# Three components of an edge vector, read as 96 rows of their own in the message stage of a four-layer graph network

## The reference

```python
sender, receiver = edge_index
s, v = node_feats[:, :32] @ W_up_s, einsum('nui,uw->nwi', node_feats[:, 32:].reshape(n, 32, 3), W_up_v)
tpw = silu(silu(edge_feats @ A1 + b1) @ A2 + b2) @ A3        # four weights of 32 for each edge
w0, w1, w2, w3 = split(tpw, 4)
ss, vs = s[sender], v[sender]
y_s, y_v = edge_attrs[:, :1], edge_attrs[:, 1:4]             # a scalar and three vector components
out_s0 = ss * y_s * w0
out_s3 = einsum('eui,ei->eu', vs, y_v) / sqrt(3) * w3
out_v1 = ss[:, :, None] * y_v[:, None, :] * w1[:, :, None]   # the three components, each times 32 channels
out_v2 = vs * y_s[:, :, None] * w2[:, :, None]
message = segment_sum(concat(out_s0, out_s3, out_v1, out_v2), receiver) / 10
out = message @ W_out                                        # scalar and vector parts with their own weights
```

## Time and profile before

| what | value |
|---|---|
| time before, median of 3 runs | 3766.24 us (3753.16 to 3766.95) |
| span of the profiled execution, the only time that it has | 4163.4 us |
| PE busy | 2637.4 us, 63% |
| PE weight loads | 1689.0 us, 41% |
| DVE busy | 1800.3 us, 43% |
| ACT busy | 1103.2 us, 26% |
| POOL busy | 2178.9 us, 52% |
| moved by DMA | 872.83 MB, mean 210 GB/s |
| message stage | about 2,990 to 3,690 us of the span |

### The profile page before, as it was taken

How to read it: one execution, slowest core, us unless ns; L and a number is a source line. 1 busy time by engine, 2 the same in 40 slices (tenths; PEclk the granted TensorE clock), 3 DMA queues, 4 the chain that set the end, 5 groups by cost and what they waited for, 6 DMA issues and landing times. The chain is left out here.

```text
span 4163.4 us, 41911 instructions
## 1 busy us (share of the span) xinstructions
PE 2637.4 (63%) x11696; PEld 1689.0 (41%) x11696; DVE 1800.3 (43%) x4207; ACT 1103.2 (26%) x2880; POOL 2178.9 (52%) x1937
## 2 busy tenths in 40 slices
PE   1547973665563648964555564359667786759696
PEld 1324653454452335643444442234323343334343
DVE  6433433554453544434444453320246685650203
ACT  0113430222232614421222233410224453430001
POOL 4357556666675757566666675620156577520000
PEclk9965555777776865556766777679778897869797
DMA  9997996777774549996777773537245564527372
GB/s 314 364 291 279 395 338 183 234 227 232 218 206 118 95 148 332 394 311 180 219 232 220 222 185 89 152 98 282 92 125 147 141 180 136 140 73 292 114 288 100
DMA packets 672304, 872.83 MB, mean 210 GB/s; under 512 B 136977, under 2 KB 557144, under 8 KB 631524
## 3 DMA queue, kind: packets, MB, share of 16 engines
q1 hardware_dynamic: 314324, 581.00, 39.8%
q0 software_dynamic: 118784, 157.05, 16.1%
q10 hardware_dynamic: 239008, 132.59, 10.8%
HBM read 441.21 MB, written 429.28 MB: 209 GB/s over the span
## 5 line engine op out<-in xcount | busy, mean ns | idle before, releaser
L1716 POOL DMA_INDIRECT att_rows<-table,kvrow x784 | 796.0, 1015 | 400.9 <-issue 230.3
L1484 POOL DMA_INDIRECT matrix<-count,place x392 | 621.5, 1585 | 279.2 <-DMA matrix<-count,place 196.9
L2119 POOL DMA_INDIRECT msg_rows<-rows,msg_src x392 | 411.4, 1050 | 448.6 <-DMA msg_src<-in_src_pt 218.1
L1774 PE MATMUL att_po<-att_message,att_mate 128*128 128x264 f32 (+1 forms) x1568 | 438.3, 419 | 300.0 <-issue 199.4
L1774 PEld LDWEIGHTS att_po<-att_message,att_mate 128*128 128x128 f32 x1568 | 296.1, 232 | 400.6 <-issue 324.9
L1607 PE MATMUL tab_bank<-wk,tab_kv 32*128 32x256 f32 x1600 | 378.6, 686 | 74.3 <-DVE tab_part L1566 43.3
L1566 DVE COPY tab_part<-tab_bank 128x512 f32<-128x512 f32 x400 | 258.2, 686 | 357.6 <-DMA table<-tab_part 249.5
L1842 ACT ACTIVATE att_out<-att_po 128x136 f32<-128x136 f32 (+1 forms) x784 | 230.0, 337 | 456.1 <-remote 241.6
L1607 PE MATMUL tab_bank<-wv,tab_kv 32*128 32x256 f32 x1600 | 332.4, 613 | 0.0
L1591 ACT ACTIVATE tab_part<-tab_bank 128x512 f32<-128x512 f32 x400 | 222.4, 594 | 367.5 <-DMA table<-tab_part 267.6
L1900 DVE TENSOR_TENSOR att_prod<-att_rows,att_pq 128x512 f32<-128x512 f32 x196 | 133.6, 682 | 419.5 <-issue 400.1
(11 more groups left out here) (399 smaller groups left out, 3970.2 us busy)
## 6 DMA issues: line engine op xcount, KB each, us to landing
table<-tab_part SPq DMA_DIRECT2D x200, 1024.0 KB
gsum_cells<-matrix SPq DMA_DIRECT2D x50, 1604.0 KB
att_sums<-att_out ACTq DMA_DIRECT2D x196, 272.0 KB
matrix<-a SPq DMA_DIRECT2D x25, 1604.0 KB
nb_cells<-matrix SPq DMA_DIRECT2D x25, 1604.0 KB
a<-query_rows SPq DMA_DIRECT2D x144, 256.0 KB
query_rows<-a SPq DMA_DIRECT2D x16, 1568.0 KB
att_message<-in_ea_rows SPq DMA_DIRECT2D x98, 256.0 KB
```

The lines of the kernel that those rows point to most:

```text
L1484: nc.gpsimd.indirect_dma_start(D.matrix, bass.IndirectOffsetOnAxis(ap=K.place[:, col:col + 1], axis=0), K.count[:, col:col + 1], None, com ...
L1716: nc.gpsimd.indirect_dma_start(rows[g % RR][:, j, :], None, D.table, bass.IndirectOffsetOnAxis(ap=K.kvrow[:, t:t + 1], axis=0)).then_inc(r ...
L1774: nc.tensor.matmul(po[j][:, 0:w], mate[h % RS][:, j, :], message[h % RM][:, j, 0:w], start=True, stop=True).then_inc(summed, 1)
L2119: nc.gpsimd.indirect_dma_start(rows[g % RR][:, j, :], None, D.rows, bass.IndirectOffsetOnAxis(ap=src[:, t:t + 1], axis=0)).then_inc(rows_i ...
```

## The change

The host now repeats each of the three components 32 times and passes an input `axes` of 96 rows and 50,176 columns (19 MB) in place of `ea4` with 4 rows. The load on SP takes a plain tile of 96 rows and 512 columns out of it. No instruction is added, removed or moved on any engine; one DMA per group has another source. The bytes that it moves are the same, 192 KB.

```diff
@@ messages, queue of SP
                 if g >= RS:
                     sp.wait_ge(graded, g - RS + 1)
-                sp.dma_start(out_y[k][32:P, :], D.ea4[1:4, g * W:(g + 1) * W].unsqueeze(1).broadcast_to([3, 32, W])).then_inc(out_y_in[k], 16)
+                sp.dma_start(out_y[k][32:P, :], D.axes[:, g * W:(g + 1) * W]).then_inc(out_y_in[k], 16)
@@ kernel, inputs made by the host
-        "ea_rows": np.ascontiguousarray(padded(given["edge_attr_128"].T, EP).T), "ea4": padded(given["edge_attr_4"].T, EP),
+        "ea_rows": np.ascontiguousarray(padded(given["edge_attr_128"].T, EP).T), "axes": np.repeat(padded(given["edge_attr_4"].T[1:4], EP), 32, axis=0),
```

## The result

| | median of the runs | ratio to the kernel before (95% interval) |
|---|---|---|
| before | 3761.92 us (6 runs, 3753.16 to 3766.95) | |
| after | 3778.15 us (6 runs, 3773.81 to 3781.76) | 1.0046 (1.0033 to 1.0060) |

What follows compares the result with a forecast made beforehand. The prediction took POOL, with its gathers, as the lasting bound of the message stage. Its terms, 0, 0, -3 us and 0, summed to -3 us against the median of 3766.2 us: 3763 us, range 3705 to 3795 us.

Steps and rivals of the forecast that it cites:

- The bound: Message stage: POOL's four gathers a group bind in the long run, at 5.0 to 6.0 us a group.
- the change cannot reach this cost: Gathers behind a DVE scan wait for its end, 0.78 us more; by the port rule the change leaves this alone.
- Term 1: Load into `msg_vec`: issued early and read eight groups later, so nobody waits for it; 0.
- Term 2: Load on three DMA engines: 5.1 to 5.8 us a group, POOL taken to bind instead; 0, at most -78 us.
- rival A: The three engines bound the timed runs: 20 to 78 us faster, 3690 to 3745 us; chance 0.23.
- Term 3: Gathers land sooner beside a spread load, paid only when the stage fills and ends; -3 us, bounds 0 and 6.4 us.
- Term 4: Source of the load: reading 96 memory rows in place of three rows 32 times, equal bytes; 0.
- Rival C: POOL's gathers meet DVE's scan more often: 27 us slower, 3793 us, at worst 77 us, 3843 us; chance 0.11.
- Forecast: Whole kernel: the main expectation of -3 us, 3763 us, within 0.5% of no change; chance 0.55.
- D: The load keeps to few engines or was on 16 before: time unchanged at 3766 us; chance 0.03.
- B: DVE's stops before `msg_vec` hang on the busy engines and shrink: 70 to 175 us faster, 3590 to 3695 us; chance 0.08.
- What would show it: Profile signs: SP's queue on 16 engines briefly, gathers keeping 1.05 us, DVE stopping before `msg_vec` some 150 to 200 us.

Runs made afterwards that it cites:

- x1: The changed kernel plus a second load of 3 x 24 rows per group on three engines into an unread tile, five store buffers; ratio 1.0088 to the kernel before.
- o1: The kernel before with DVE's scan placed ahead of the second `msg_prod`; ratio 1.0061.
- o2: The changed kernel with DVE's scan placed ahead of the second `msg_prod`; ratio 1.0062 to the kernel before.
- x3: The changed kernel with the tile `total` in PSUM in place of SBUF; ratio 0.9947 to the kernel before.
- n1: The kernel before, unchanged, timed against itself and profiled once more; ratio 0.9996.
- x2: The kernel before with the vector components loaded for the first eight groups only, 90 of 98 loads left out; ratio 1.0025.
- e2: The kernel before reading the 96 host rows with the three components as outermost dimension, so three engines carry them; ratio 0.9999.
- e3: The kernel before with its three source rows each spread over 16 engines, in three loads per group; ratio 1.0030.
- o3: The changed kernel with DVE's `msg_sc` placed ahead of the scan; ratio 0.9988 to the kernel before.
- z1: The changed kernel plus a second load of 3 x 12 rows per group on three engines into an unread tile; ratio 1.0034 to the kernel before.
- w6: The changed kernel with its 96 rows laid out in six blocks, so six engines carry 16 rows each; ratio 1.0048 to the kernel before.
- w12: The changed kernel with its 96 rows laid out in twelve blocks of 8 rows, so 12 engines; ratio 1.0038 to the kernel before.

## Why the prediction was right or wrong

- **The bound.** Right. "The lasting bound of the stage is POOL" orders the runs: the five with gathers below 385 us are the five fastest (0.9915 to 0.9947), the nine above 415 us the nine slowest (1.0025 to 1.0088). It is not the whole of x1, o1 and o2, which lost more than their gathers did. The rule that it quoted from the Trainium skill (SBUF — State Buffer, section "SBUF: two separate sides") holds too, for operands in SBUF: x3 took one of the two away and the blocking went. The Trainium skill says there that whichever side starts first holds the ports for its whole instruction and the other waits; here only the gather was seen to wait, until 0.76 us behind the end of the scan, and the scan kept its 1.27 us, also where a gather had begun up to 0.2 us ahead of it (19 times in n1). The sentence "the change cannot reach this cost" drew too much from the rule. The rule says that gather and scan take turns, not how often they meet.
- **Term 1, waiting for the load: 0.** Right. `msg_vec` waits for no DMA in the profile after. Leaving the 175.2 us of stops out of the sum was right also; they were in one profiled execution only, and what made them was not tried.
- **Term 2, three engines: 0.** Right, and with it rival A is out: with the load off these engines (x2) nothing became faster.
- **Term 3, "gathers land sooner: -3 us … paid once when the stage fills and once when it ends". This is the step that failed**, and not by its size alone. They do land sooner, by 1.3 us (3.96 to 2.70 us). It is not paid once, though: in these traces DVE waits for the landing in 71 groups (53 before; the rows of the waits above), so the landing sets where DVE's scan stands against POOL's next gathers, in each of these. The reason given, "since POOL runs ahead", was read from the one long profile: there DVE waited for gathered rows 4 times in all and POOL 82.3 us for DVE's `msg_sc`, as the stops had put DVE behind; in the kernel before, repeated, that is 4.9 us. It also goes against the prediction's own bound, since an engine that bounds the stage doesn't stay ahead. In place of -3 us it is 424.4 - 406.0 = +18.4 us of gathers, of which 16 show in the time.
- **Term 4, reading 96 rows: 0.** Right (e2: 0.9999). So is the issue on SP, which fell by 442 ns a load for nothing.
- **Rival C was the case**, "POOL meets the scan more often", with a chance of 0.11. Its mechanism is right; its price was 27 us, and measured were 16. It reckoned with one full meeting of 0.78 us in each group; in the trace the gather comes 0.67 us into the scan and pays 0.42 us. The prediction had in the earlier trace rows the gather that starts ahead of the scan and the one that starts behind it. Which of the two a shift of 1 us gives was not to be read from there, but that the shift would act in each group was: DVE's stock runs out, as the text says itself, and then it waits for landings. "By luck", as C puts it, is right so far: no rule found here says beforehand which shift is a bad one.
- **A's price and the chances.** "0.2 to 0.8 us a group" does not follow from the sums: 5.8 - 5.0 gives 0.8, but the upper values (5.8 and 6.0) and the middle ones (5.45 and 5.5) leave nothing for A. Forecast and D add up to 0.58, where the text has 0.57 for "same", and "slower" has 0.12 with C at 0.11 "apart from its smallest cases".
- **B and D** are out: the stops were not the load's, and the spread did change (landing, issue time, e3).
- **"What would show it."** The 16 engines for a short time are there (SP's queue rests 44% of the stage). "Gathers keep 1.05 us" and "DVE still stops for some 150 to 200 us" are both wrong (1.083 us; 8.7 us for the same row). "I am wrong if the time moves by more than 19 us while POOL's total stays" didn't catch the case, as POOL's total moved.

**What stays open.** Why the old spread is the good one among those tried (3, 6, 12, 16 engines, none) has no rule; the small model had the wrong sign for o3. With DVE's order as it was, all spreads but the old one land after 2.4 to 2.9 us and cost 0.25 to 0.48%, and the old one lands after 3.9 us; nothing clean lies between, since x1 and z1, made to move the landing by itself, didn't do so. So the landing is supported, by o1 and o2 above all, and not shown by a run that moves it alone. Shown are: it is the number of engines, it acts through longer gathers, they are long because of DVE's operands in SBUF, and DVE's order alone takes the difference away.

## What to carry to other kernels

A load that nobody waits for can still change the time, since it moves when other transfers land, and with that the phase between two engines that disturb each other; so a hidden load that is spread over all engines is not free by itself. Where gathers on POOL bound a stage, sum their durations and look at which DVE instruction each long one begins in; then give that instruction one operand in PSUM (0.65% here), before anything is tuned by order or by spread, since a gain from phase alone may go with the next edit. When a profile's span is far above the median of the timed runs, take a second one before explaining its waits.

## What the runs showed that I had not expected

- A gather that begins inside a DVE scan with two SBUF operands ends 0.76 us behind it, inside such a multiply 0.82 us behind it, and DVE's scan keeps its 1.27 us. With one operand of the scan in PSUM the gather takes its 0.944 us.
- Less traffic was slower: 90 loads of 192 KB left out, +0.25% (x2).
- The issue of a load on SP takes 760 ns for the broadcast and 318 ns for the plain rows, of the same bytes. It isn't the broadcast: e2, with the rows in three blocks of 32 and nothing repeated, takes 759 ns, w6 774 and w12 829.
- One kernel, two profiled executions: 4163.4 and 3766.4 us, with 175.2 and 8.1 us of `issue` stops before `msg_vec`.
